# Two head groups of a causal attention accumulated into one bank of outputs through zero-padded value columns

## The chip, the cores and the metric

One core of a Trainium2 chip runs the whole kernel. The metric is the device time of one execution in microseconds (us), the median of three runs.

## The reference

A block of four batches of 512 tokens with 128 features. After a layer norm two branches are added to the input: an attention over chunks of 16 tokens (local and dilated), called the local attention below, and a second branch with a low-rank causal attention over all 512 tokens of a batch (16 heads of 8 features) and a mixture of experts. The change is in the causal attention:

```python
k = (kv_lat @ W_ku).reshape(B, S, NH, HH); q = (q_lat @ W_qu).reshape(B, S, NH, HH)
v = (kv_lat @ W_vu).reshape(B, S, NH, HD)
...
scores = jnp.einsum('bqhd,bkhd->bhqk', qq, kk) * scale
scores = jnp.where(causal[None, None], scores, jnp.finfo(scores.dtype).min)
probs = jax.nn.softmax(scores, axis=-1)
y = jnp.einsum('bhqk,bkhd->bqhd', probs, v).reshape(B, S, H)
return y @ W_o
```

## The kernel before, in words

**One list of steps, five engines.** `plan()` writes out one list of 760 steps. Every engine walks this list in order and does its part of each step, so the order of the list is the order of work on each engine; engines wait for each other by semaphores. Lists for the parts (scores, local attention, projections, stacks of queries and keys, experts and so on) are interleaved by `merged`, each spread evenly over stretches given in the table `SPREAD`.

**Banks.** Seven of the eight PSUM banks are in three rings: A (2 banks: score maxima, local scores, the experts' last product), B (3: scores for the exponentials, the experts' first products) and M (2: nearly everything else). A step takes the next bank of its ring and waits until the step that had this bank before has been drained. The eighth, `bank_c`, collects the products of probabilities and values.

**The causal attention.** The 16 heads of a batch go in four groups of four. For a group there are ten S steps (scores into bank A, L1215 and masks L1222; VectorE takes the row maxima, L1068), one SHIFT (the maxima are transposed, L1303, rounded in two parts, L1075 and L1076, and sent by DMA into the query stack), ten E steps (transposed scores into bank B, L1236; ScalarE's exponential into `p_mla`, L886) and four PV steps (L1332, one for each tile of 128 keys). A PV step has four matmuls, one for each head of the group: head m of group g has its own 32 partitions of `bank_c`, and the weights are 32 columns of `v_mla` from the head's nine on (eight values and a one, which gives the softmax's denominator); the other columns of the 32 leave unused rows. E and PV of a group run two groups behind S.

**Output of a group.** After the last PV step ScalarE copies `bank_c` to `oT_mla` (L895). Then, three or four E steps into the next group, comes the step Y: TensorE transposes `oT_mla` in four tiles into a bank M (L1339), VectorE takes the reciprocals of the denominators (L1130) and multiplies (L1131) into `y_mla`, which lies in `lat_room`. TensorE's first PV step of the next group waits for ScalarE's copy (`c_drained`). So there are 16 Y steps, four for each batch. After the fourth come YT (transposes, L1344) and X1 (the output projection, L1349). The values themselves come from step MV: four matmuls (L1283), which ScalarE copies into `v_mla` (L786).

**Which head is in which group.** VectorE lays the weights of queries and keys out in step WF by sixteen small copies (L981 to L985); the head order of the stacks follows from them. Before, group g holds heads 4g to 4g + 3.

**The start.** GpSimd (POOL) clears `half`, `k_part`, `q_part` and sets `v_rows` to one (L676 to L679), then takes the square roots of the first batch's statistics (L665, in `root`), for which it waits for VectorE; VectorE goes on with L955 to L957, L1000, the normalised rows `xr` (L1002), WF, `xn` (L988), L993, L994, and two memsets, of `s_loc` (L996) and of the ones in `v_mla` (L997). GpSimd's next work in the list is L747. ScalarE's first MV drain waits for `ones_set` at 2.

## Time and profile before

| | us |
|---|---|
| median of three runs | 392.73 |
| the three runs | 392.72, 392.73, 394.63 |
| span of the profiled execution, first to last instruction | 387.9 |

The page gives the profiled execution by its span alone; the median stands 4.8 us above that span. PE is TensorE's matmuls, PEld its weight loads, DVE VectorE, ACT ScalarE, POOL GpSimd, SP the engine whose queue issues most DMAs. The span has three parts: a start (to about 64 us), a stretch in which causal attention, local attention and projections of different batches overlap (64 to about 298 us), and the experts (to the end). "Idle before, releaser" tells what ended an engine's idle time.

### The profile page before, as it was taken

The page shows a single profiled execution, that of the slowest core. Times are in us where ns is not written, and L with a number is a line of the kernel's source. Part 1 is how long each engine was busy: PE and PEld are TensorE (multiplying, and loading weights), DVE is VectorE, ACT ScalarE, POOL GpSimd, SP SyncE. Part 2 cuts the span into 40 slices and gives each one's busy share as a digit, 9 for nine tenths or more (in the row PEclk, how much of TensorE's full clock was granted, in tenths as well). Part 3 has the DMA queues.
Part 4 walks back from the last instruction along what each step waited for, and adds up shares of the span by engine and source line. Part 5 has one row for each costly group of instructions (what it writes and reads, how often), then busy time and mean ns, then how long its engine had stood idle before and what let it go on. Part 6 is the DMA issues. An engine that isn't in the chain of part 4 may idle for free.

```text
span 387.9 us, 11664 instructions
## 1 busy us (share of the span) xinstructions
PE 337.9 (87%) x4504; PEld 205.0 (53%) x4504; DVE 286.0 (74%) x720; ACT 224.1 (58%) x545; POOL 122.7 (32%) x148
## 2 busy tenths in 40 slices
PE   5678987898898988998688889878999999999994
PEld 4366654454465445464445455445445755665663
DVE  6987668798666898878679978879623569668644
ACT  4356434676576465664467658656665564746462
POOL 6286407210600472603301400000201365444543
PEclk9988998999999999999999999999999999999998
DMA  8453141333105033350211331206000000000100
GB/s 193 82 197 100 26 155 43 89 56 65 27 22 160 24 69 54 84 167 3 64 41 30 58 65 48 43 6 161 3 2 0 3 0 27 3 28 0 30 0 27
DMA packets 29141, 21.84 MB, mean 56 GB/s; under 512 B 12312, under 2 KB 26008, under 8 KB 29048
## 3 DMA queue, kind: packets, MB, share of 16 engines
q1 hardware_dynamic: 28872, 20.91, 21.9%
q8 instruction: 36, 0.59, 0.6%
q10 hardware_dynamic: 216, 0.20, 0.2%
q14 instruction: 17, 0.14, 0.1%
HBM read 6.81 MB, written 6.19 MB: 34 GB/s over the span
## 4 chain that ended last, share of the span: by engine, by line
PE 48%; DVE 28%; ACT 10%; issue 7%; SPq 3%; DMA 1%; ACTq 1%; POOL 1%; DVEq 0%; POOLq 0%
PE bank_B L1428 11%; DVE neg_max L1068 6%; PE bank_c L1332 6%; PE bank_A L1434 5%; PE bank_B L1236 5%; PE bank_A L1374 5%; ACT p_mla L886 3%; DVE s_loc L1085 2%; DVE row_max L1082 2%; ACT k_diag L830 2%; PE bank_M L1272 2%; SPq L624 1%; PE bank_M L1382 1%; DVE k_diag L1193 1%; PE bank_M L1397 1%
## 5 line engine op out<-in xcount | busy, mean ns | idle before, releaser
L886 ACT ACTIVATE p_mla<-bank_B 128x512 f32<-128x512 f32 (+1 forms) x176 | 94.3, 562 | 62.7 <-PE bank_B L1222 61.9
L1068 DVE TENSOR_REDUCE neg_max<-bank_A 128x1 f32<-128x512 f32 (+3 forms) x176 | 108.6, 637 | 19.5 <-PE bank_A L1222 15.8
L1236 PE MATMUL bank_B<-q_stack,k_stack 54*128 54x512 bf16 (+3 forms) x256 | 63.2, 303 | 10.9 <-DVE neg_max L1068 5.1
L1215 PE MATMUL bank_A<-k_stack,q_stack 52*128 52x512 bf16 (+3 forms) x256 | 63.7, 303 | 0.1
L1428 PE MATMUL bank_B<-xrT,k_diag 128*128 128x512 f32 x128 | 61.7, 600 | 1.2 <-DVE k_diag L1193 1.0
L759 POOL TENSOR_TENSOR x<-x,q_part 128x512 f32<-128x512 f32 x31 | 39.4, 1272 | 61.3 <-ACT q_part L920 43.0
L1332 PE MATMUL bank_c<-p_mla,v_mla 128*32 128x128 f32 (+12 forms) x512 | 47.5, 444 | 5.6 <-ACT p_mla L886 5.5
L1236 PEld LDWEIGHTS bank_B<-q_stack,k_stack 54*128 54x128 bf16 x256 | 19.2, 93 | 54.0 <-issue 23.1
L920 ACT ACTIVATE q_part<-bank_A,expert_w 128x128 f32<-128x128 f32 x108 | 30.8, 368 | 28.8 <-PE bank_A L1434 28.8
L1193 DVE SCALAR_TENSOR_TENSOR k_diag<-k_diag,bank_B 128x512 f32<-128x512 f32 x32 | 22.0, 687 | 31.5 <-ACT k_diag L904 30.3
L1222 PE MATMUL bank_A<-masks 64*128 64x64 bf16 (+2 forms) x352 | 43.1, 202 | 0.0
L1222 PE MATMUL bank_B<-masks 64*128 64x64 bf16 (+2 forms) x352 | 43.1, 201 | 0.0
L1434 PEld LDWEIGHTS bank_A<-k_diag 128*128 128x128 f32 x256 | 32.8, 191 | 14.4 <-issue 14.3
L1222 PEld LDWEIGHTS bank_B<-masks 64*128 64x128 bf16 x352 | 32.7, 96 | 12.6 <-issue 0.3
L1434 PE MATMUL bank_A<-k_diag 128*128 128x128 f32 x256 | 34.0, 276 | 0.7 <-DVEq L1201 0.7
L1222 PEld LDWEIGHTS bank_A<-masks 64*128 64x128 bf16 x352 | 32.9, 96 | 1.7
L1428 PEld LDWEIGHTS bank_B<-xrT,k_diag 128*128 128x128 f32 x128 | 21.4, 191 | 18.4 <-issue 12.0
L665 POOL TENSOR_TENSOR nrm<-nrm,half 128x8 f32<-128x8 f32 (+1 forms) x8 | 10.6, 1330 | 64.0 <-DVE nrm L1144 61.6
L1374 PE MATMUL bank_A<-k_diag,q_part 128*32 128x128 f32 x544 | 21.4, 292 | 3.6 <-DVE neg_max L1068 1.3
L1198 DVE TENSOR_TENSOR k_diag<-bank_B,k_diag 128x512 f32<-128x512 f32 x32 | 22.1, 691 | 1.1
L771 POOL CAST parts<-rot 128x512 bf16<-128x512 f32 x6 | 3.7, 609 | 56.2 <-DVE rot L1049 52.5
L1082 DVE TENSOR_REDUCE row_max<-bank_A 128x32 f32<-128x512 f32 (+1 forms) x20 | 12.7, 635 | 11.6 <-PE bank_A L1374 11.5
(150 smaller groups left out, 568.8 us busy)
## 6 DMA issues: line engine op xcount, KB each, us to landing
v_dram<-v_rows SPq DMA_DIRECT2D x12, 324.0 KB, 3.6
k_stack<-parts SPq DMA_DIRECT2D x48, 64.0 KB
q_stack<-parts SPq DMA_DIRECT2D x45, 64.0 KB
k_diag<-k_part SPq DMA_DIRECT2D x48, 34.0 KB
v_diag<-v_dram SPq DMA_DIRECT2D x32, 45.0 KB, 2.1
v_diag<-v_dram SPq DMA_DIRECT2D x32, 36.0 KB, 2.1
v_dram<-v_rows SPq DMA_DIRECT2D x4, 283.5 KB, 2.8
x<-in_x SPq DMA_DIRECT2D x4, 256.0 KB, 8.0
```

The lines of the kernel that those rows point to most:

```text
L759: link(nc.gpsimd.tensor_tensor(x[:, tb, :], x[:, tb, :], weighted[down_no[step] % 2], ALU.add))
L886: drained_by(nc.scalar.activation(p_of(n)[:, m:m + len(heads), 0:w], src, ACT.Exp, scale=SCALE), step)
L920: ins = nc.scalar.activation(weighted[n % 2][:, i, :], down[:, i, :], ACT.Copy, scale=expert_w[:, c * NT + i, e - 1:e])
L1068: drained_by(nc.vector.tensor_reduce(neg_max[:, g, m:m + len(heads), i], src, AX.X, ALU.max, negate=True), step)
L1193: drained_by(nc.vector.scalar_tensor_tensor(out=hid[n % 2], in0=gate[n % 2], scalar=1.0, in1=bank_of(step + (0,))[:], op0=ALU.add, op1=ALU ...
L1215: return nc.tensor.matmul(bank_of(step)[:, n * w:(n + 1) * w], q_stack[b % 2][rows, h % 8, i * P:(i + 1) * P], k_stack[b % 2][rows, h % 8, ...
L1222: return nc.tensor.matmul(to, half_eye[half, low, :], triangle[half, :].unsqueeze(1).broadcast_to((SLOT, len(heads), SLOT)), start=False, ...
L1236: nc.tensor.matmul(bank_of(step)[:, m * w:(m + 1) * w], k_stack[b % 2][rows, h % 8, j * P:(j + 1) * P], q_stack[b % 2][rows, h % 8, j * P: ...
L1332: last = nc.tensor.matmul(bank_c[32 * m:32 * m + width, j * P:], heads[:, first:first + width], p_of(n)[:, m, 0:S - j * P], start=(j == 0) ...
L1374: last = nc.tensor.matmul(bank[PAIR * j:PAIR * j + PAIR, c:c + P], q_part[:, a, pair, :], k_diag[:, a, :, CHUNK * pair:CHUNK * pair + CHUN ...
L1428: full_by(nc.tensor.matmul(bank_of(use)[:], w_exp[:, e, m, :], x2T[:, c, :], start=True, stop=True), use)
L1434: last = nc.tensor.matmul(bank[:, i * D:(i + 1) * D], hid[n % 2][:, i * P:(i + 1) * P], w_exp[:, e, 2, :], start=True, stop=True)
```

## The change

The 16 heads are regrouped: group g holds heads g, 4 + g, 8 + g and 12 + g, by another reading order in the sixteen copies of WF. Each head has 18 columns in `v_mla`: nine zeros, its eight values and a one (and one more cell of zeros at the end). Groups 0 and 1, and groups 2 and 3, now accumulate in one `bank_c`. The weights of an even group start at the head's values, so that its result is in rows 0 to 8 of the 32 partitions; those of an odd group start at the nine zeros, so that its result is in rows 9 to 17, and each adds zeros to the other's rows. ScalarE's copy and the step Y are done after the odd group only: 8 in place of 16, each with 32 reciprocals and 256 products a partition in place of 16 and 128. The even Y steps are filtered out after `merged`, so the other steps keep their order; the ring M is dealt out anew without them. GpSimd zeroes `v_mla` (2 x 4 x 17 x 18 = 2448 floats a partition) and sets 128 ones behind its first square roots; VectorE's memset of ones goes.

```diff
-    steps += merged(*lists)
+    steps += [step for step in merged(*lists) if step[0] != "Y" or step[2] % 2]
...
-        v_mla = sb("v_mla", [P, 2, NT, H, HD + 1])
+        v_mla = sb("v_mla", [P, 2, NT, H + 1, 2 * (HD + 1)])
...
+        y_places = lat_room[:, 0:NT * D].rearrange("p (n r) -> p n r", r=PV_WIDTH)
-        rden_mla = sb("rden_mla", [P, H])
+        rden_mla = sb("rden_mla", [P, 2 * H])
...
             root(1, range(1))
+            nc.gpsimd.memset(v_mla[:], 0.0).then_inc(v_mla_zeroed, 1)
+            pool.wait_ge(v_mla_zeroed, 1)
+            nc.gpsimd.memset(v_mla[:, :, :, 0:H, 2 * HD + 1:], 1.0).then_inc(ones_set, 1)
...
-                    drain(step, v_mla[:, b % 2, :, :, 0:HD], bank[:].rearrange("p (i h d) -> p i h d", i=NT, h=H))
+                    drain(step, v_mla[:, b % 2, :, 0:H, HD + 1:2 * HD + 1], bank[:].rearrange("p (i h d) -> p i h d", i=NT, h=H))
...
-                elif kind == "PV" and step[3] == NT - 1:
+                elif kind == "PV" and step[3] == NT - 1 and step[2] % 2:
                     _, b, g, _ = step
                     act.wait_ge(pv_done, pv_no[step])
-                    if g != GROUP_ORDER[0]:
-                        wait_full(act, ("Y", b, GROUP_ORDER[GROUP_ORDER.index(g) - 1]))
+                    if g == 3:
+                        wait_full(act, ("Y", b, 1))
                     elif b:
-                        wait_full(act, ("Y", b - 1, GROUP_ORDER[-1]))
+                        wait_full(act, ("Y", b - 1, 3))
                     nc.scalar.copy(oT_mla[:], bank_c[:]).then_inc(c_drained, 1)
...
-                    ku, qu, rq = (bank[:, 64 * n:64 * n + 64].rearrange("p (e a d) -> p e d a", e=2, d=HH) for n in range(3))
+                    ku, qu, rq = (bank[:, 64 * n:64 * n + 64].rearrange("p (m e b d) -> p e d b m", m=4, e=2, d=HH)
+                                  for n in range(3))
...
-                    nc.vector.memset(v_mla[:, :, :, :, HD:], 1.0).then_inc(ones_set, 1)
...
                     link(nc.vector.reciprocal(den, o[:, :, :, HD]))
+                    c = HD * (g - 1)
                     drained_by(nc.vector.tensor_tensor(
-                        y_mla[:, :, 4 * HD * g:4 * HD * g + 4 * HD].rearrange("p i (h d) -> p i h d", h=4), o[:, :, :, 0:HD],
-                        den.unsqueeze(3).broadcast_to((P, NT, 4, HD)), ALU.mult), step)
+                        y_places[:, :, c:c + 2 * HD].rearrange("p n (a d) -> p n a d", a=2), o[:, :, :, 0:HD],
+                        den.unsqueeze(3).broadcast_to((P, H, 2, HD)), ALU.mult), step)
...
-                    if j == 0 and n > 1:
-                        pe.wait_ge(c_drained, (n - 1) // NT)
+                    second = g % 2
+                    if j == 0 and not second and n > 1:
+                        pe.wait_ge(c_drained, (n - 1) // (2 * NT))
                     heads = v_mla[:, b % 2, j].rearrange("p h d -> p (h d)")
                     for m in range(4):
-                        first = (HD + 1) * (4 * g + m)
-                        width = min(PV_WIDTH, H * (HD + 1) - first)
+                        first = (HD + 1) * (2 * (4 * m + g) + 1 - second)
+                        width = min(PV_WIDTH, 2 * (HD + 1) * (H + 1) - first)
                         last = nc.tensor.matmul(bank_c[32 * m:32 * m + width, j * P:], heads[:, first:first + width],
-                                                p_of(n)[:, m, 0:S - j * P], start=(j == 0), stop=(j == NT - 1),
+                                                p_of(n)[:, m, 0:S - j * P], start=(j == 0 and not second),
+                                                        stop=(j == NT - 1 and second == 1),
                                                 skip_group_check=True)
```

## Rows read from the trace of the kernel before

**Rows 1.** The page's part 1: busy us, share of span, instructions.

```profile
PE 337.9 (87%) x4504; PEld 205.0 (53%) x4504; DVE 286.0 (74%) x720; ACT 224.1 (58%) x545; POOL 122.7 (32%) x148
```

**Rows 2.** Busy time of PE, PEld, DVE, ACT, POOL by stretch; clock, DMA share, GB/s.

```profile
64.00:282.00 218.00, 189.33 (x3404) 110.30 (x3404) 176.17 (x450) 135.00 (x326) 49.57 (x71) 0.99 0.25 61
302.00:388.00 86.00, 79.97 (x376) 49.92 (x374) 54.71 (x125) 47.77 (x143) 40.44 (x32) 0.99 0.04 13
```

**Rows 3.** The page's part 4: the chain that ended last, by engine.

```profile
PE 48%; DVE 28%; ACT 10%; issue 7%; SPq 3%; DMA 1%; ACTq 1%; POOL 1%; DVEq 0%; POOLq 0%
```

**Rows 4.** Who waited for whom: us in total, times, longest us.

```profile
PEld bank_B L1236 <- DVE neg_max L1068: 20.4, 43, 1.5
```

**Rows 5.** Instructions by line and form: busy us, mean ns, idle before.

```profile
L1085 DVE TENSOR_TENSOR s_loc<-bank_A,row_max 128x512 f32<-128x512 f32 x16 | 11.1, 692 | 0.5
...
L1339 PE MATMUL bank_M<-eye,oT_mla 128*128 128x128 f32 x64 | 10.3, 284 | 0.9 <-ACT pT_loc L867 0.8
...
L895 ACT COPY oT_mla<-bank_c 128x512 f32<-128x512 f32 x16 | 9.3, 583 | 0.5 <-PE bank_c L1332 0.5
...
L1096 DVE RECIPROCAL rden<-bank_M 128x32 f32<-128x32 f32 x16 | 5.6, 349 | 0.4 <-DVE s_loc L1085 0.2
...
L1131 DVE TENSOR_TENSOR lat_room<-bank_M,rden_mla 128x128 f32<-128x128 f32 x16 | 4.7, 292 | 0.6
...
L1130 DVE RECIPROCAL rden_mla<-bank_M 128x16 f32<-128x16 f32 x16 | 4.0, 249 | 7.0 <-PE bank_M L1339 6.8 <-DVE s_loc L1085 0.2
```

**Rows 6.** The same view: matmuls of values with 32 and with 9 columns.

```profile
L1332 PE MATMUL bank_c<-p_mla,v_mla 128*32 128x512 f32 x104 | 17.0, 605 | 0.6 <-ACT p_mla L886 0.6
...
L1332 PE MATMUL bank_c<-p_mla,v_mla 128*9 128x512 f32 x8 | 4.1, 596 | 0.0
```

**Rows 7.** The chain that ended last, in order of time: start us, us, what.

```profile
79.86 0.59 PE bank_M L1339 x4
...
144.73 0.17 DVE rden_mla L1130
...
144.93 0.30 DVE lat_room L1131
...
283.91 0.58 ACT oT_mla L895
```

**Rows 8.** Timeline of POOL in the start: start us, us, instruction, idle before.

```profile
1.98 1.92 POOL L678 MEMSET q_part<- 128x2176 f32 x1
3.95 1.18 POOL L679 MEMSET v_rows<- 128x1296 f32 x1
5.71 1.66 POOL L665 TENSOR_TENSOR nrm<-nrm,half 128x8 f32<-128x8 f32 x1 [0.58 <-DVE nrm L949]
15.82 1.15 POOL L747 TENSOR_TENSOR rest<-rot,parts 128x512 f32<-128x512 f32 x1 [8.46 <-ACT parts L841]
```

**Rows 9.** Timeline of DVE in the start.

```profile
4.71 0.44 DVE L947 TENSOR_SCALAR nrm<-mv 128x4 f32<-128x4 f32 x1
...
7.61 0.17 DVE L956 TENSOR_SCALAR nrm<-nrm 128x4 f32<-128x4 f32 x1
...
12.88 0.17 DVE L997 MEMSET v_mla<- 128x128 f32 x1
```

**Rows 10.** Timeline of all engines near 322 us, its rows of POOL and DVE.

```profile
321.78 1.26 POOL L759 TENSOR_TENSOR x<-x,q_part 128x512 f32<-128x512 f32 x1 [0.71 <-ACT q_part L917]
321.85 0.18 DVE L1150 RECIPROCAL nrm<-nrm 128x4 f32<-128x4 f32 x1
...
322.07 1.26 DVE L1152 TENSOR_SCALAR xn<-x,nrm 128x128 f32<-128x128 f32 x2
```

**Rows 11.** Line L1152 alone: ns min/median/max, first and last start us.

```profile
L1152 DVE TENSOR_SCALAR xn<-x,nrm x16: 274/279/1061, 163.8 to 323.4; 128x128 f32<-128x128 f32 x16
```

**Rows 12.** Columns as in rows 2: two stretches of 2 us in the start.

```profile
22.00:24.00 2.00, 0.58 (x5) 0.33 (x6) 0.93 (x7) 1.33 (x3) 1.81 (x4) 0.99 0.43 129
24.00:26.00 2.00, 2.00 (x10) 2.00 (x11) 1.81 (x3) 0.14 (x2) 1.65 (x5) 0.50 0.51 151
```

More of the change, by code:

```diff
@@ L461, in build @@
         ones_set = sem("ones_set")
+        v_mla_zeroed = sem("v_mla_zeroed")
         pT_cleared = sem("pT_cleared")
@@ L975, in _, with to @@
                     wait_full(dve, step)
-                    ku, qu, rq = (bank[:, 64 * n:64 * n + 64].rearrange("p (e a d) -> p e d a", e=2, d=HH) for n in range(3))
-                    rk = w_ropek.rearrange("p (e a) d -> p e d a", e=2)
+                    ku, qu, rq = (bank[:, 64 * n:64 * n + 64].rearrange("p (m e b d) -> p e d b m", m=4, e=2, d=HH)
+                                  for n in range(3))
+                    rk = w_ropek.rearrange("p (m e b) d -> p e d b m", m=4, e=2)
+                    def to(n, d0, d1, e):
+                        return w_mla[:, n, d0:d1, :, e].rearrange("p d (b m) -> p d b m", m=4)
                     part = HH // 2
@@ L980, in _ @@
                         for side, plain, turn in ((0, ku, rk), (1, qu, rq)):
[L981 to L985 removed]
+                            nc.vector.tensor_copy(to(side, 0, HH, e), plain[:, e])
+                            nc.vector.tensor_copy(to(side, HH, HD, e), turn[:, e])
+                            nc.vector.tensor_copy(to(2, HH * side, HH * side + part, e), turn[:, e, part:])
+                            nc.vector.tensor_copy(to(2, HH * side + part, HH * side + HH, e), turn[:, e, 0:part])
                     drained_by(nc.vector.tensor_copy(w_mla_v[:], bank[:, 192:192 + D]), step)
@@ L1120, in _ @@
                 elif kind == "Y":
-                    g, n = step[2], GROUP_ORDER.index(step[2])
-                    o = bank[:].rearrange("p (i h r) -> p i h r", i=NT, h=4)
+                    g = step[2]
+                    o = bank[:].rearrange("p (n r) -> p n r", r=PV_WIDTH)[:, :, 0:2 * (HD + 1)].rearrange(
+                        "p n (a c) -> p n a c", a=2)
                     wait_full(dve, step)
-                    if n:
-                        wait_drained(dve, ("Y", b, GROUP_ORDER[n - 1]))
+                    if g == 3:
+                        wait_drained(dve, ("Y", b, 1))
                     elif b:
                         wait_full(dve, ("YT", b - 1))
-                        wait_drained(dve, ("Y", b - 1, GROUP_ORDER[-1]))
-                    den = rden_mla[:].rearrange("p (i h) -> p i h", i=NT)
+                        wait_drained(dve, ("Y", b - 1, 3))
+                    den = rden_mla[:].rearrange("p (n a) -> p n a", a=2)
                     link(nc.vector.reciprocal(den, o[:, :, :, HD]))
+                    c = HD * (g - 1)
                     drained_by(nc.vector.tensor_tensor(
-                        y_mla[:, :, 4 * HD * g:4 * HD * g + 4 * HD].rearrange("p i (h d) -> p i h d", h=4), o[:, :, :, 0:HD],
-                        den.unsqueeze(3).broadcast_to((P, NT, 4, HD)), ALU.mult), step)
+                        y_places[:, :, c:c + 2 * HD].rearrange("p n (a d) -> p n a d", a=2), o[:, :, :, 0:HD],
+                        den.unsqueeze(3).broadcast_to((P, H, 2, HD)), ALU.mult), step)
                 elif kind == "X1":
@@ L1336, in _ @@
                 elif kind == "Y":
-                    pe.wait_ge(c_drained, b * (H // 4) + GROUP_ORDER.index(step[2]) + 1)
+                    pe.wait_ge(c_drained, 2 * b + step[2] // 2 + 1)
                     for i in range(NT):
```

4 lines of the change are left out of this document (removed).

## The prediction

> **What bounds the kernel now.** I read the page's busy shares first, then the busy time by stretch, then the chain that ended last, and last the rows of the instructions that the change touches. The reader is to see that no engine is full over the span, TensorE nearest to it at 87% [rows 1]. Between 64 and 282 us TensorE is busy 189.3 of 218 us, VectorE 176.2 and ScalarE 135.0; in the experts (302 us on) TensorE has 80 of 86 us and the others some 50 [rows 2]. The chain lies to 48% on TensorE, 28% on VectorE and 10% on ScalarE [rows 3]: in the overlapped stretch TensorE and VectorE hand the bound to and fro, as the weight loads of E show, which waited 20.4 us for VectorE's maxima in 43 places [rows 4]. So neither engine's saving counts in full; what counts is what lies on the chain, and whether the other engine's saving falls at the same place.
>
> **What is removed in the overlapped stretch.** Eight Y steps and the copies before them.
> TensorE: 64 transposes kept it busy for 10.3 us in union [rows 5]; half is 5.2 us (0.65 us a step). The matmuls of values keep their number; for the last heads some had 9 to 27 columns of weights and now all have 32, and the rows give 605 ns against 596 [rows 6], so nothing: eight narrow ones at 9 ns more are 0.1 us.
> ScalarE: 8 copies of 583 ns, 4.7 us [rows 5].
> VectorE: a Y costs 249 + 292 = 541 ns, two cost 1.08 us. After, one costs a reciprocal of 32 elements, 349 ns by L1096, and a product of 256. Between 128 elements (292 ns) and 512 (692 ns, L1085) a straight line gives 292 + 128 x 1.04 = 425 ns. That is 0.77 us for a pair, so 0.31 us is saved, 2.5 us for eight [rows 5]. The new output has gaps of 16 floats and its input gaps in the bank; L1131's had both, so I add nothing, and 10% more would be 0.3 us in all.
> The wait of TensorE's first PV for the copy goes in eight places, and in ring M each step after a removed Y now waits for an older one. I found no place where the first wait ended an idle time, and the second is bounded by 0 and about 1 us; I take 0.3.
>
> **How much of it is on the chain.** I went through the chain around each of the eight. Three removed Ys have their transposes on it, 0.59 us each (one of the three is the piece at 79.86), 1.8 us. Three have VectorE's two instructions on it, 0.17 + 0.30 and the handovers, about 0.5 us each (one is the pair at 144.73 and 144.93), 1.5 us. A seventh, near 267 us, has 0.4 us of VectorE, and the eighth has the copy at 283.91, 0.58 us. Sum 4.3 us [rows 7]. The eight Ys that stay are longer by 0.77 - 0.54 = 0.23 us; three of them have this same pair of instructions on the chain, 0.7 us back. So the chain gets 3.6 us shorter. Other paths run close to it: VectorE alone is relieved by 2.5 us only, TensorE alone by 5.2. I take 3.3 us, with the 0.3 of ring M in it, and keep 2.0 and 5.5 (TensorE's 5.2 and a bit of ring M) as the ends. The experts after 302 us are unchanged and only start earlier; TensorE is nearly full there [rows 2], so nothing is given back.
>
> **What is added in the start.** ScalarE's copies into `v_mla` and WF's sixteen copies keep their sizes, only strides change: nothing, at worst 0.2 us. VectorE loses a memset of 0.17 us [rows 9], which lies on its unbroken row of work: 0.17 us gained. GpSimd gets two memsets behind its square roots. From 2176 elements in 1.92 us and 1296 in 1.18 [rows 8] comes 0.84 ns an element and 0.09 fixed, so 2448 elements take 2.15 us. They start at about 7.44 (the roots end at 5.71 + 1.66 = 7.37) and end at 9.6; the 128 ones end by 9.9. GpSimd's next work is at 15.82, after 8.46 us idle [rows 8], so for GpSimd and for the wait of the first MV drain this is hidden.
> It is not hidden for VectorE. In the start L947, a tensor_scalar of four elements, took 0.44 us where the like L956 took 0.17 [rows 9]; it began at 4.71 and ended at 5.15, just behind GpSimd's memset of `v_rows`, which ended at 3.95 + 1.18 = 5.13 [rows 8]. The same near 322 us: GpSimd's L759 runs from 321.78 to 323.04. A reciprocal beside it took its 0.18 us, but two tensor_scalars of L1152, begun at 322.07, took 1.26 [rows 10]; one of this line took 1061 ns where the median is 279 [rows 11], and 322.07 + 1.06 is 323.13. So a tensor_scalar from SBUF to SBUF that comes during an instruction of GpSimd waits for its end, while a reciprocal does not. In the new kernel L956 comes at 7.61, 0.17 us into the memset. It then ends at 9.6 in place of 7.78, 1.8 us late, and all that follows on VectorE to 20 us (the rows `xr`, WF, `xn`, the rotations) is one unbroken row of work in the chain. ScalarE, TensorE and GpSimd wait for it there, so the start gets longer by 1.8 - 0.17 = 1.7 us, rounded up. The low end is the stretch that L947 itself showed, 0.44 - 0.17 = 0.27 us, less the 0.17: 0.1. The high end adds a memset that takes longer than the line, 2.2 us.
> The Trainium skill states this as a rule (SBUF — State Buffer, section Who interferes with whom): an instruction of VectorE in a mode with two ports, which tensor_scalar can enter, shares a port pair with GpSimd, and the one that comes second is fully blocked until the other is done. By this rule the added time is the whole rest of the memset and the start 1.7 us longer; were rows 9 only a slow first instruction, the sum would be 1.6 us better. The trace agrees with the rule in both places.
>
> **Sum.** 392.7 - 3.3 + 1.7 = 391.1; in the profile, a span of 387.9 - 1.6 = 386.3 us, with the same 4.8 us around it by which the median stands above the span. I say **391.0**. A change of 0.5%, 2.0 us, is about what a measurement of this kernel can tell from none, so the bounds are 390.8 and 394.7.
>
> **The rivals.**
> *The start costs nothing* (the memset begins late or between VectorE's instructions, or the delay is taken up later): 392.7 - 3.3 - 0.2 = 389.2. For it: nothing in the rows but a chance of timing; if VectorE came first, L1002, also a tensor_scalar and three instructions later, would meet the memset and wait the same. Chance 0.12.
> *TensorE is the bound everywhere*: its whole 5.2 us and 0.3 of ring M count, with the start as above: 392.7 - 5.5 + 1.7 = 388.9. For it, 87% busy in the stretch; against it, the 20.4 us of waits for VectorE. Chance 0.15.
> *VectorE is the bound in the stretch*: only its 2.5 us count, less some for rows on its own that wait: 392.7 - 2.0 + 1.7 = 392.4. Chance 0.20.
> *Slower: the late start lets TensorE's clock fall.* Behind a stretch of 2 us with 0.58 us of matmuls the granted clock went to 0.50, its lower level of 1.2 GHz, for the next 2 us [rows 12]. TensorE now waits 1.8 us longer before the transposes of `xr`. If the clock falls there, the first transposes and the four projections of 512 columns behind them run at half speed and, as VectorE waits for each, cost up to 2 us; later dips of the same kind, at other places than now, could cost 2 us more. With the low saving: 392.7 - 2.0 + 1.7 + 3 = 395.4. It decides once the clock costs more than 2.3 us over the low saving, or 3.6 over mine. Against it: before those steps TensorE runs warm-up matmuls and the clock holds now through comparable gaps. Chance 0.08.
> That the change does not do what it says (the steps stay) can be left out: the Y steps are filtered from the list.
>
> **How the numbers follow.** My forecast has 0.45, with its own range of 390.0 to 392.3; a third of that lies below 390.8. Faster by over 0.5%: 0.12 + 0.15 + 0.15 of the forecast's 0.45 = 0.42. Slower: 0.07 of the last rival, which can also end short of the bound. Same: the rest, 0.51. The range of 388.6 to 393.0 takes in the first three rivals and leaves out the last and the tails of the others.
>
> **What would show it.** Right: 32 instructions each on L1339's successor (half of 64), 8 copies to `oT_mla` with 583 ns, reciprocals of 128x32 near 350 ns and products of 128x256 near 425; a tensor_scalar of about 2 us on VectorE at 7.6 us beside a GpSimd memset of 2.15 us, and the first rotation (L1017) at about 14.6 in place of 12.9; the experts start some 1.6 us earlier, and from there the two kernels are alike. Wrong: L956 at 0.17 us with the memset beside it; TensorE's idle time between 64 and 298 us growing by as much as its work shrinks (then it was VectorE's bound); a granted clock below 1.0 before 20 us; PV matmuls slower than 605 ns; ScalarE's first copy into `v_mla` waiting for the ones.

## The result and the profile after

| kernel | median us | runs | mean clock |
|---|---|---|---|
| before, measured beside it | 393.68 | 4 | |
| changed | 400.74 | 4 (398.13 to 404.38) | 0.956 |
| ratio to before | 1.0174, 95% interval 1.0087 to 1.0260 | | |

The changed kernel is slower by 1.7% in these runs. The forecast was 391.0 in a range of 388.6 to 393.0. Here and below a ratio leaves out the slow runs, those more than 1.5% above the quickest run of their kernel, while a mean is over all runs, since the runs of one kernel spread here without a step.

The page after: busy time, the granted clock in 40 slices, and the chain by engine.

```profile
PE 346.9 (87%) x4472; PEld 206.8 (52%) x4472; DVE 285.8 (72%) x703; ACT 221.5 (56%) x537; POOL 125.1 (31%) x150
...
PEclk9996999999699998999999989999979999999998
...
PE 47%; DVE 22%; SPq 11%; ACT 8%; issue 6%; POOL 3%; DMA 2%; DVEq 0%; ACTq 0%; POOLq 0%
```

Against [rows 1]: TensorE has 32 matmuls fewer and yet 9.0 us more busy time, which is a lower clock and not more work. Against [rows 3]: VectorE's share of the chain went from 28% to 22%, and that of SPq, the time in which SyncE issues DMAs one after another, from 3% to 11%. The span is 397.6 us, the execution 399.42.

The changed lines, by form:

```profile
L1352 PE MATMUL bank_M<-eye,oT_mla 128*128 128x128 f32 x32 | 5.2, 285 | 0.8 <-ACT pT_loc L872 0.8
L900 ACT COPY oT_mla<-bank_c 128x512 f32<-128x512 f32 x8 | 4.7, 581 | 0.5 <-PE bank_c L1344 0.5
L1142 DVE TENSOR_TENSOR lat_room<-bank_M,rden_mla 128x256 f32<-128x256 f32 x8 | 3.4, 424 | 0.3
L1140 DVE RECIPROCAL rden_mla<-bank_M 128x32 f32<-128x32 f32 x8 | 2.8, 350 | 3.5 <-PE bank_M L1352 3.3 <-DVE s_loc L1094 0.2
L791 ACT COPY v_mla<-bank_M 128x512 f32<-128x512 f32 x4 | 2.6, 656 | 6.9 <-PE bank_M L1294 6.9
```

All the work that the change removes is gone, and the forecasts of 349 and 425 ns hold. Only the copy into `v_mla`, with 72 bytes from head to head in place of 36, took 656 ns where before's (its L786) took 586: 0.3 us for four, forecast at 0 to 0.2.

The start, POOL's and then DVE's timeline:

```profile
7.42 2.14 POOL L684 MEMSET v_mla<- 128x2448 f32 x1
9.62 0.33 POOL L686 MEMSET v_mla<- 128x128 f32 x1
```

```profile
7.40 0.18 DVE L960 RECIPROCAL nrm<-nrm 128x4 f32<-128x4 f32 x1 [1.84 <-POOL nrm L667]
7.61 1.97 DVE L961 TENSOR_SCALAR nrm<-nrm 128x4 f32<-128x4 f32 x1
9.62 0.18 DVE L962 RECIPROCAL nrm<-nrm 128x4 f32<-128x4 f32 x1
```

The tensor_scalar of four elements was held for 1.97 us, to the memset's end, as forecast. The Trainium skill (SBUF — State Buffer, section Who interferes with whom) says that of a GpSimd instruction and a VectorE instruction in a mode with two ports, which tensor_scalar can enter, the one that comes second is fully blocked; this trace agrees, with 1.97 us in place of the 0.17 of [rows 9].

Behind that the changed kernel's profiled execution loses more than forecast. The second instruction of each SHIFT (L1076, after it L1085) marks the progress of the overlapped stretch; it starts at these times in the profiled executions (us from the start; e1 is the first experiment below):

```
SHIFT number        1      3      4      5      6      10      16    span
before          48.04  78.88  90.14 100.89 117.70  186.82  276.18   387.9
changed         51.17  82.03  92.72 105.01 123.42  193.43  283.00   397.6
e1              48.72  79.64  90.33 102.50 119.67  188.96  281.40   396.0
```

The changed kernel is 3.1 us late at the first SHIFT, not 1.7; then, where the forecast had it catch up by 3.3 us, it falls back by another 3.7 to the sixteenth, and by 2.9 from there to the end, where the granted clock is low between 292 and 300 us.

One pair of executions can't give the start's price, though. The transposes of `xr` come at 11.20 to 11.24 us in all four profiles with the memset (changed, e2, e3, e8) and at 9.39 to 9.69 in the fourteen without it: 1.8 us that the memset surely costs. The first SHIFT comes at 48.7 to 55.3 us (mean 51.6) in the four, and at 45.9 to 53.2 (mean 49.9) in the fourteen.

**Which execution the forecast stood on.** In nearly all executions measured since, of before too, the time is 1.8 us above the span (399.42 and 397.6 here; up to 2.4 in one kernel). The 4.8 us between before's span and its median were thus most likely not time around the span: that execution will have been one of some 389.7 us (387.9 + 1.8), at a mean clock of 0.984, while 63 runs of the kernel before, those beside e1 to e8, e13 and e14, had a mean of 394.2 at 0.973 and reached from 388.6 to 402.8 (with the 18 runs beside the other experiments the mean is 394.0). So a profile says where time goes in one execution; small differences need means over many.

### The profile page after: what moved, and what is told of

Same layout as the page of the kernel before. It is cut to its first block, busy times and chain, and to the rows that moved or that the text cites. A ratio compares the mean times of both kernels' runs of the same rounds, so it can differ in the third digit from the quotient of the medians.

```text
span 397.6 us, 11553 instructions
## 1 busy us (share of the span) xinstructions
PE 346.9 (87%) x4472; PEld 206.8 (52%) x4472; DVE 285.8 (72%) x703; ACT 221.5 (56%) x537; POOL 125.1 (31%) x150
## 4 chain that ended last, share of the span: by engine, by line
PE 47%; DVE 22%; SPq 11%; ACT 8%; issue 6%; POOL 3%; DMA 2%; DVEq 0%; ACTq 0%; POOLq 0%
PE bank_B L1441 11%; PE bank_c L1344 6%; SPq L542 5%; PE bank_A L1447 5%; SPq L626 5%; PE bank_B L1247 5%; DVE neg_max L1077 5%; PE bank_A L1387 4%; ACT p_mla L891 3%; PE bank_M L1283 2%; DVE s_loc L1094 2%; DVE row_max L1091 2%; DMA q_stack<-shift 2%; PE bank_M L1288 1%; PE bank_M L1278 1%
## 5 line engine op out<-in xcount | busy, mean ns | idle before, releaser
L1247 PE MATMUL bank_B<-q_stack,k_stack 54*128 54x512 bf16 (+3 forms) x256 | 65.5, 312 | 12.2 <-DVE neg_max L1077 5.3
L1226 PE MATMUL bank_A<-k_stack,q_stack 52*128 52x512 bf16 (+3 forms) x256 | 66.0, 312 | 2.0 <-DVE neg_max L1077 2.0
L1441 PE MATMUL bank_B<-xrT,k_diag 128*128 128x512 f32 x128 | 63.7, 615 | 0.9 <-DVE k_diag L1204 0.8
L1344 PE MATMUL bank_c<-p_mla,v_mla 128*32 128x128 f32 (+3 forms) x512 | 49.2, 457 | 6.2 <-ACT p_mla L891 6.2
L1233 PE MATMUL bank_A<-masks 64*128 64x64 bf16 (+2 forms) x352 | 44.4, 206 | 0.0
L1233 PE MATMUL bank_B<-masks 64*128 64x64 bf16 (+2 forms) x352 | 44.3, 206 | 0.0
L1233 PEld LDWEIGHTS bank_B<-masks 64*128 64x128 bf16 x352 | 33.6, 98 | 13.8 <-issue 1.9
L1233 PEld LDWEIGHTS bank_A<-masks 64*128 64x128 bf16 x352 | 33.8, 98 | 2.2 <-issue 0.8
L1226 PEld LDWEIGHTS bank_A<-k_stack,q_stack 52*128 52x128 bf16 x256 | 19.4, 94 | 5.5 <-DVE neg_max L1077 2.2
```

The costliest lines, as they stand in the source:

```text
L1226: return nc.tensor.matmul(bank_of(step)[:, n * w:(n + 1) * w], q_stack[b % 2][rows, h % 8, i * P:(i + 1) * P], k_stack[b % 2][rows, h % 8, ...
L1233: return nc.tensor.matmul(to, half_eye[half, low, :], triangle[half, :].unsqueeze(1).broadcast_to((SLOT, len(heads), SLOT)), start=False, ...
L1247: nc.tensor.matmul(bank_of(step)[:, m * w:(m + 1) * w], k_stack[b % 2][rows, h % 8, j * P:(j + 1) * P], q_stack[b % 2][rows, h % 8, j * P: ...
L1344: last = nc.tensor.matmul(bank_c[32 * m:32 * m + width, j * P:], heads[:, first:first + width], p_of(n)[:, m, 0:S - j * P], start=(j == 0 ...
L1441: full_by(nc.tensor.matmul(bank_of(use)[:], w_exp[:, e, m, :], x2T[:, c, :], start=True, stop=True), use)
```

## The experiments

Changed and before differ by about 6 us in their means. The theories were: **the start** (memset, and what the late start does), **the removal** is worth less than forecast since something else ends the waits (SP's queue), **the layout** (padded columns) costs, and **the clock** falls more often where TensorE has less to do. Means are given with their standard errors, and ratios with their 95% intervals against runs of before on the same chip. I read differences of a few us from the means, with 394.2 +- 0.4 for before (63 runs). The experiments ran in five groups, each on a chip of its own with runs of before beside it, whose means were 393.4 (e1 to e4), 394.4 (e5 to e8), 392.5 (e9 to e12), 395.1 (e13, e14) and 393.8 (e15, e16), with errors of 0.5 to 0.8. Against its own group e1 is 2.1 +- 0.9 us over before, e2 4.2 +- 1.2, e7 1.6 +- 1.0 and e8 5.9 +- 1.4.

### e8_changed_again: the changed kernel once more

No edit.

> The changed kernel once more, for its spread beside the others. All theories: 398 to 402, and 3 to 6 us above the first run's kernel.

Median 400.48 (13 runs, 393.97 to 407.73, mean 400.3 +- 1.2, clock 0.959), ratio 1.0070 (1.0003 to 1.0137). Slower again; the two ratios, 1.0174 and 1.0070, show how far few runs of this kernel carry. The mean is 6.1 +- 1.3 over before's.

### e1_scalar_zero: the change without GpSimd's memset

```diff
-            nc.gpsimd.memset(v_mla[:], 0.0).then_inc(v_mla_zeroed, 1)
...
+            nc.scalar.memzero(v_mla[:].rearrange("p s j h c -> p (s j h c)")).then_inc(v_mla_zeroed, 1)
...
+                    dve.wait_ge(v_mla_zeroed, 1)
+                    nc.vector.memset(v_mla[:, :, :, 0:H, 2 * HD + 1:], 1.0).then_inc(ones_set, 1)
```

> The changed kernel, but ScalarE zeroes v_mla in its idle time behind its two clears, and VectorE sets the ones where the kernel before did, so that no GpSimd memset meets VectorE's tensor_scalar. Theory A (the loss is the late start and what it does to TensorE's clock there, later dips are chance): the tensor_scalar takes 0.17 us again, the start is as before and the time is 3 us under the kernel before, about 390. Theory B (less work on TensorE lets its clock fall more often): the start is as before, but dips near 102, 153, 231 and 293 us stay, and the time is 395 to 398.

Median 395.72 (12 runs, mean 395.5 +- 0.7, clock 0.966), ratio 1.0070 (1.0024 to 1.0116). The first SHIFT comes at 48.72, 0.7 us behind before. So by the means the memset on GpSimd costs 400.3 - 395.5 = 4.8 +- 1.4 us of the changed kernel; a line through each kernel's runs, read at the same clock of 0.975, gives 395.5 - 392.9 = 2.6 us, so that nearly half of it is clock. Against each one's own group of runs it is 5.9 - 2.1 = 3.8 +- 1.6. The ratios, 1.0070 for both kernels, show no difference at all. What is left is still above before by 1.3 +- 0.8 us, without the memset: the removal does not pay. At the clock of 0.975 before stands at 393.4, e1 0.5 us under it.

### e2_before_late: the kernel before with only the memset

```diff
+        room = sb("room", [P, 2448])
...
             root(1, range(1))
+            nc.gpsimd.memset(room[:], 0.0).then_inc(room_zeroed, 1)
+            pool.wait_ge(room_zeroed, 1)
```

> The kernel before with one GpSimd memset of 2448 floats into a room of its own behind the first square roots; nothing else changed. Theory A: VectorE's tensor_scalar takes 2.0 us, the first score step is 3 us later and the time is 3 us or more above the kernel before, 396 to 400, with the same dips moved or added as in the changed kernel. Theory B: 1.8 us slower and no new dips after 60 us, 394.5 to 396.

Median 398.24 (12 runs, mean 397.6 +- 1.1, clock 0.968), ratio 1.0059 (1.0006 to 1.0113), by the means 3.4 +- 1.2 us over before. DVE's and PE's timelines in its start:

```profile
7.61 1.97 DVE L960 TENSOR_SCALAR nrm<-nrm 128x4 f32<-128x4 f32 x1
```

```profile
11.20 1.11 PE L1271 MATMUL bank_M<-eye,xr 128*128 128x128 f32 x4 [2.75 <-DVE xr L1006]
12.11 1.06 PE L1252 MATMUL bank_c<-eye 128*128 128x128 f32 x4
13.25 3.75 PE L1281 MATMUL bank_M<-xrT,w_mla 128*128 128x512 f32 x4
```

The kernel before had for the same three 0.66, 0.61 and 1.96 us. TensorE sat idle for 2.75 us before the transposes of `xr`, where it was 0.93, and then ran at half speed; the granted clock is below 1.0 from 10 to 18 us. The first SHIFT is at 51.36, 3.3 us late, and every later interval is that of before within 0.1 us: the sixteenth is at 279.47. So in this execution the start costs 1.8 us of blocked VectorE and another 1.5 of slow TensorE, and both persist. This is the last rival's first half, at its place and near its price ("up to 2 us"). But TensorE is also slow there in nine of the fourteen profiles without the memset (e1's lines stand at the end): the transposes of `xn`, which follow these projections, come at 18.0 to 19.2 us in the four profiles with it (mean 18.9) and at 15.8 to 17.3 in the fourteen without (mean 16.2; before 15.79). On average that is 1.8 us and another 0.8.

### e7_left_out: the removal without the layout

The kernel before with its own values, weights and banks; the even Y steps and the copies before them are left out and the odd ones take two groups' size, so the results of groups 0 and 2 are lost.

```diff
+    steps += [step for step in merged(*lists) if step[0] != "Y" or step[2] % 2]
...
-                    if j == 0 and n > 1:
-                        pe.wait_ge(c_drained, (n - 1) // NT)
+                    if j == 0 and g % 2 == 0 and n > 1:
+                        pe.wait_ge(c_drained, (n - 1) // (2 * NT))
```

> The kernel before with its own layout of values and heads; the copies and Y steps of groups 0 and 2 are left out (the results of these groups are lost), those of groups 1 and 3 have the changed kernel's larger form. So it has the whole saving and nothing of the padding. Theory C: as the first run, 394 to 397, since neither has the new wait lifted. A theory E, that the padded layout costs time by itself (copies into v_mla, weights of 32 columns, another order of heads): 390 to 392.

Median 395.62 (12 runs, mean 395.9 +- 0.8, clock 0.968), ratio 1.0061 (0.9999 to 1.0124): the same as e1 within 0.4 +- 1.0 us. Padded columns, strides, regrouped heads and ScalarE's zeroing cost nothing that can be told; leaving the steps out is by itself worth nothing, or less. The line through e7's runs stands at 394.3 at the clock of 0.975, 0.9 us over before's, where e1's is 0.5 under: the removal's worth at equal clock is nil within this scatter.

### e3_filler and e4_zero_filler: TensorE's work put back alone

In place of each removed Y four products of `eye` with itself go into a bank of ring M, drained by VectorE's queue without an instruction; once in the changed kernel, once in e1.

```diff
+                elif kind == "FILL":
+                    for i in range(NT):
+                        last = nc.tensor.matmul(bank[:, i * P:(i + 1) * P], eye[:], eye[:], start=True, stop=True)
+                    full_by(last, step)
```

> The changed kernel with four products of the unit matrix with itself on TensorE, into a bank of ring M, in the place of each Y that was removed; nothing reads them. Theory B: TensorE is kept busy as before, the clock's dips behind 90 us go, and the time falls to 393 to 396 although TensorE has more to do. Theory A: nothing changes in the dips, the time stays at 400 or grows by up to 3 us.

> Both edits: zeroes by ScalarE and the filler on TensorE. Only ScalarE's copies and VectorE's part of the removed Ys are then saved. Theory A: between the kernel before and the first run, 391 to 392. Theory B: 391 to 392 too, but below the first run. If the first run is faster than this one, the removed transposes are worth their time.

Medians 398.47 (6 runs, mean 399.4 +- 1.1, clock 0.973) and 399.26 (6, 399.5 +- 0.7, 0.967). In the changed kernel the products cost nothing (399.4 against 400.3), in e1 they cost 4.0 +- 1.0 us. So it isn't that TensorE merely needs to be kept busy: the profiles still have falls of the clock, e3's at 194 us and e4's at 100. Why the products cost e1 so much isn't shown; that at the old places they lay on the chain is my reading. The two kernels differ only in where `v_mla` is zeroed, and here GpSimd's memset costs nothing: 399.4 against 399.5, -0.1 +- 1.3 us.

### Where the removal's gain went

e1 against before by intervals between SHIFTs (us, from the same marks; the last column adds up to e1's 4.46 us more from the third SHIFT to the sixteenth):

```
interval   before     e1   difference   granted clock in e1
3 to 4      11.26  10.69     -0.57      full
4 to 5      10.75  12.17     +1.42      falls at 100
5 to 6      16.81  17.17     +0.36      low until 104
6 to 10     69.12  69.29     +0.17      full
10 to 11    18.93  20.73     +1.80      falls at 195
11 to 14    41.55  41.65     +0.10      full
14 to 15    18.74  20.15     +1.41      falls at 253
15 to 16    10.14   9.91     -0.23      full
```

Two things are in it, SP's queue and the clock. Where the clock stays full, the sum of the differences is -0.5 us: that is what the removal of some seven Y steps was worth at equal clock (0.66 us from SHIFT 12 to 13 went the other way, and e7 has the same 17.12 us there, e1 17.11, before 16.45).

The queue shows first behind SHIFT 4. SP's timeline with the DMAs of the second and the fourth SHIFT, and TensorE's wait for the latter, in before and then in e1:

```profile
65.56 1.20 SPq L632 DMA_DIRECT2D q_stack<-shift  x2
94.57 1.21 SPq L632 DMA_DIRECT2D q_stack<-shift  x2
98.13 0.37 PE L1236 MATMUL bank_B<-q_stack,k_stack 54*128 54x512 bf16 x1 [1.07 <-DMA q_stack<-shift]
```

```profile
66.23 1.20 SPq L634 DMA_DIRECT2D q_stack<-shift  x2
95.23 1.21 SPq L634 DMA_DIRECT2D q_stack<-shift  x2
99.11 0.37 PE L1247 MATMUL bank_B<-q_stack,k_stack 54*128 54x512 bf16 x1 [1.85 <-DMA q_stack<-shift]
```

Between the two SP issues DMAs with no pause over 0.11 us, and the distance is 29.0 us whether the Y steps are there or not (29.00 also in changed and in e2, 29.02 in e7). e1 had gained 0.57 us from SHIFT 3 to 4 and lost it, and more, in that wait: 0.8 of the 1.42 us from SHIFT 4 to 5 are before the clock falls. The transposes at 79.86 in [rows 7] lay on the chain, and yet leaving them out could gain nothing here, since behind them the chain of before runs through this queue, from 83.86 to 95.15 us.

The stretch from 6 to 10 holds four batch-quarters of work and gained nothing. Its chain, e1 from 134 us on (in order of time, us):

```profile
148.24 0.69 SPq L626
...
148.97 0.69 SPq L626
...
149.69 0.64 SPq L542
150.38 0.65 SPq L542
...
151.07 0.61 SPq L542
...
151.72 0.58 SPq L634
...
152.35 2.69 DMA q_stack<-shift
...
155.17 0.37 PE bank_B L1247
```

These are the last of an unbroken row that begins at 134.63. SP issues the DMAs of key stack, query stack and `k_diag` at 0.61 to 0.75 us each, one after another; the SHIFT's two, for which VectorE's last instruction ran at 142.7, go at 151.72, and TensorE waits 0.6 us for their landing. The kernel before has the same row, from SP's timeline:

```profile
139.71 2.05 SPq L540 DMA_DIRECT2D q_stack<-parts  x3
141.81 5.85 SPq L624 DMA_DIRECT2D k_diag<-k_part  x8
147.70 1.99 SPq L540 DMA_DIRECT2D q_stack<-parts  x3
149.73 1.21 SPq L632 DMA_DIRECT2D q_stack<-shift  x2
```

There the SHIFT's instruction ran at 140.66 and its DMAs were issued at 149.73; the row up to there lasts 17.15 us, in e1 17.09. TensorE reached this one late enough, but not by much. Its waits for SHIFT's DMAs in the whole execution (us in total, times, longest), first before, then e1, e7, e11 and e12:

```profile
PE bank_B L1236 <- DMA q_stack<-shift: 1.1, 1, 1.1
```

```profile
PE bank_B L1247 <- DMA q_stack<-shift: 2.4, 2, 1.9
```

```profile
PE bank_B L1240 <- DMA q_stack<-shift: 3.6, 4, 2.0
```

```profile
PE bank_B L1241 <- DMA q_stack<-shift: 5.8, 4, 3.4
```

```profile
PE bank_B L1252 <- DMA q_stack<-shift: 8.0, 4, 3.2
```

Where TensorE comes earlier it waits longer for the same queue.

### e11_before_more and e12_zero_more: more work on SP's queue

Two more DMAs of 1 KB ahead of each SHIFT's, 32 issues in all, in before and in e1.

```diff
+                    for r in range(2):
+                        sp.dma_start(spare[:, 2 * (4 * b + g) + r, :], io["c_eye"][0:4 * NT, 0:16]).then_inc(spare_in, 16)
```

> The kernel before with two more small DMAs on SP's queue (1 KB each, into a spare tile that nobody reads) ahead of those of each SHIFT: 32 issues, some 19 us more of SP's time. Theory C: where SP's queue is full, between the second and the tenth SHIFT above all, intervals grow by up to 1.2 us each, and TensorE waits longer for SHIFT's DMA: 4 to 10 us slower. Theory D: nothing beyond 1 us.

> The same two DMAs in the first run's kernel. Theory C: it ends level with the eleventh run at the same clock, since both are then bound by the same queue: the intervals between SHIFTs in the full stretches differ by under 0.3 us. Theory D: as the first run.

402.31 and 403.19 (2 runs each), ratios 1.0241 (1.0154 to 1.0327) and 1.0263 (1.0184 to 1.0341). 32 issues of 0.60 to 0.70 us are 19 to 22 us on SP, and about 8 us of them come through (402.3 - 394.2; 403.2 - 395.5; for e11 it is 9.9 against its own group's 392.5), in the kernel before too. Not all of this is the wait itself: e11's clock was 0.956, and its profile has some 17 us at the low clock between the first and the last SHIFT, where before's has 3. But in stretches at the full clock its intervals are longer too, from SHIFT 8 to 9 by 1.6 us (14.32 against 12.71) and by 0.4 each from 3 to 4 and from 7 to 8. So this queue is at the bound in places and next to it in others, in both kernels. With it lengthened, the removal is worth nothing again, within an error of 1.3 us.

### e9_before_kd_pool and e10_zero_kd_pool: less work on SP's queue

GpSimd issues the sixteen `k_diag` DMAs of a batch in place of SP, in before and in e1.

```diff
-                            sp.dma_start(view(k_diag[rows, 0, places[0], :],
...
+                                pool.dma_start(view(k_diag[rows, 0, places[0], :],
```

> The kernel before with the 16 DMAs for k_diag of each step KD (batches 1 to 3) issued by GpSimd, which already waits for the same local scores there, instead of by SP. SP has 48 issues of 0.7 us less. Theory C (SP's queue of issues is next to the bound before the change and is the bound after it): the waits of TensorE for the DMAs of SHIFT go (1.1 us before), and in stretches at the full clock the intervals between SHIFTs get shorter by 0 to 3 us in all; if GpSimd's issues are dear, the local scores wait instead. Theory D (the clock alone): intervals at the full clock as before.

> The first run's kernel with the same edit. Theory C: its intervals between SHIFTs at the full clock are 0.3 to 1 us shorter for each removed Y than those of the ninth run, and its time is 1 to 4 us under the ninth run's. Theory D: the intervals at the full clock differ from the ninth run's by under 0.2 us, as those of the first run from the kernel before did.

400.32 (4 runs, ratio 1.0172, 1.0106 to 1.0238) and 399.63 (5 runs, 1.0175, 1.0115 to 1.0235). TensorE's waits for the SHIFT's DMA are gone from both profiles, and from the third SHIFT to the sixth, where neither clock falls, e10 takes 37.14 us and e9 38.21: with the queue out of the way the removal is worth 1.1 us there, where with it e1 was 1.2 us behind before (clock included); the forecast was 3.3 for the whole. The DMAs of the second and fourth SHIFT are then 24.9 us apart in e9, in place of 29.0. But GpSimd pays for it, in e9 its timeline shows

```profile
143.56 2.22 POOL L720 DMA_DIRECT2D k_diag<-k_part  x4 [0.29 <-POOL q_part L729]
```

four times over, 0.55 us a DMA, and the interval from SHIFT 7 to 8, where most of them stand, took 18.45 us in e9 and 19.66 in e10 against before's 14.61, some of it by a fall of the clock in it. The bound only moved.

### e5_zero_shift_act and e6_before_shift_act: a miss

```diff
+                elif kind == "SHIFT":
...
+                    for r in range(2):
+                        act.dma_start(q_stack[b % 2][row + r:row + r + 1, a0:a0 + 4, :].rearrange("o a (i n) -> o (a i) n", n=P),
+                                     shift[:, r, :]).then_inc(shift_in[g], 16)
```

> The first run's kernel (zeroes by ScalarE), and the two small DMAs of each step SHIFT, from shift into q_stack, are issued from ScalarE's queue, no longer from SP's behind its batches of DMAs for k_diag and the stacks. Theory C (the removed Ys save nothing between 64 and 280 us because SP's queue of issues, which they leave as it is, became the bound): against the same edit of the kernel before this kernel saves 2 to 4 us, where without the edit it was no faster than the kernel before. Theory D (TensorE's clock alone eats the saving): the two kernels with this edit stand as those without, this one 1 to 3 us slower.

> The kernel before with the DMAs of SHIFT issued from ScalarE's queue. Theory C: SP's queue is only just off the bound here, so 0 to 3 us faster than the kernel before, less ScalarE's time for 32 issues. Theory D: no difference beyond ScalarE's issues, 0 to 2 us slower.

422.9 and 419.3 us, ratios 1.0625 (1.0506 to 1.0744) and 1.0640 (1.0576 to 1.0705). ScalarE's own waits in e6:

```profile
ACT p_mla L886 <- issue: 16.1, 12, 2.2
```

In before there is no such line. As I read it, ScalarE is held in its own order by the SHIFT, with the exponentials queued behind it. With a clock of 0.925 and 0.937 the two kernels are some 26 us slower, with and without the removal, which tells nothing of SP's queue.

### The clock

The second thing in the table: three falls within the stretch cost e1 some 1.0, 1.6 and 1.4 us. (Of the 1.42 and 0.36 us beside the first, 0.8 is the wait for the DMA; of the 1.80 beside the second, 0.24 is there at the full clock too, as changed and e12 show with 19.18 and 19.17 us.) At 195 us the place can be read; the windows of before, then of e1 (columns as in [rows 2]):

```profile
188.00:190.00 2.00, 2.00 (x100) 1.63 (x90) 1.36 (x3) 0.47 (x1) 0.00 (x0) 1.00 0.11 26
190.00:192.00 2.00, 0.74 (x17) 0.42 (x4) 1.62 (x6) 0.00 (x1) 0.00 (x0) 1.00 0.42 110
192.00:194.00 2.00, 1.27 (x14) 1.12 (x14) 0.11 (x1) 0.58 (x1) 0.00 (x0) 1.00 0.40 77
194.00:196.00 2.00, 2.00 (x29) 0.93 (x26) 1.47 (x3) 1.47 (x4) 0.00 (x0) 1.00 0.44 89
```

```profile
190.00:192.00 2.00, 2.00 (x94) 1.64 (x96) 1.36 (x3) 0.63 (x2) 0.00 (x0) 1.00 0.07 13
192.00:194.00 2.00, 0.63 (x33) 0.54 (x20) 1.72 (x6) 0.00 (x0) 0.00 (x0) 1.00 0.42 114
194.00:196.00 2.00, 1.16 (x9) 0.95 (x8) 0.27 (x2) 0.58 (x1) 0.00 (x0) 0.89 0.33 62
196.00:198.00 2.00, 2.00 (x14) 0.92 (x17) 1.16 (x2) 0.64 (x2) 0.00 (x0) 0.50 0.37 72
```

It is the end of a batch, where TensorE waits for the last Y's product (before 1.14 us, e1 1.37 by PE's timeline), transposes, waits for a copy (0.84) and goes on to X1. The Y that stays is 0.23 us longer, as forecast, and stands just before this gap. In e1 the granted clock then goes to 0.50, the lower level of 1.2 GHz; in before it stayed at 1.00. Before's windows there are nearly as thin, so this pair doesn't show why. At 100 us TensorE had 1.02 and 0.89 us of work in two windows of 2 us in e1, and 0.83 and 1.87 in before, whose wait was shorter. In all, the clock is below full for about 10 us of before's profiled execution (and at its end), for some 30 of the changed one's.

The other profiles say how regular this is. From SHIFT 4 to 5 the clock falls in all five profiles with the removal, with SP's queue as it was or longer, and without added products (changed, e1, e7, e8, e12), and not in before, e2, e9 and e10; it falls in e11, the kernel before with the longer queue. So here the fall goes with the wait for the DMA. From 10 to 11 it falls in e1, e7, e8 and e10, not in changed and e12, and in none of before, e2, e9 and e11. Between 64 and 76 us it is the other way: it falls in each of these last four, and with the removal in changed, e1 and e8 only. Behind the last SHIFT (290 to 308 us) it falls in changed, e1, e8 and e10, not in e7 and e12, nor in before, e2, e9 and e11. These are single executions of each kernel: a tendency, not a rule.

### e13 and e14, e15 and e16: products in the gaps

Extra products of `eye` at these places: before YT, X1, an E at 100 us and the E steps of the last group. e13 (on e1) and e14 (on before) put them into the steps' own banks, e15 and e16 those of YT and X1 into `bank_c`, ahead of the wait for a bank.

```diff
+                if kind in ("YT", "X1"):
+                    for _ in range(gap_warm(step)):
+                        nc.tensor.matmul(bank_c[:, 0:P], eye[:], eye[:], start=True, stop=True)
```

> The first run's kernel with products of the unit matrix in TensorE's gaps, each into the bank that the step behind it already owns and overwrites: four ahead of the waits of YT and two of X1 (batches 0 to 2), six ahead of the wait for SHIFT's DMA near 98 us, one in each E step of the last group. Theory F (the removed Ys widened gaps in front of which TensorE's clock now falls, and this gives the rest of the saving back): the falls near 100, 195, 253 and 291 us go, the mean clock rises from 0.966 to 0.975 or more, and the time is 390 to 393, under the first run's 395.7. Otherwise (the falls come by chance wherever they come): clock and time as in the first run, 395 to 397.

> The same products in the kernel before. Theory F: its gaps at these places seldom cost it the clock, so the mean clock rises little (0.975 to 0.98) and the time stays within 1.5 us of the kernel before. If it falls by more than 2 us, the gaps were a cost of the kernel before as well.

> As the thirteenth run, but the products ahead of YT (four) and X1 (three) go into bank_c, which is free there, and ahead of the wait for the step's own bank, so that they lie inside the gap and not behind it; five ahead of SHIFT's DMA near 98 us; one each in the first four E steps of the last group only. Theory F: no falls of the clock near 100, 195 and 253 us, mean clock 0.972 or more, and with the products now hidden 391 to 394. If the products still cost as much as the falls, 396 or more.

> The same products in the kernel before: 392 to 395 by theory F, within 2 us of the fifteenth run, since at an equal clock the removed Ys were worth about 0.5 us between the second and the last SHIFT.

| | median us | runs | mean clock | ratio |
|---|---|---|---|---|
| e13, on e1 | 399.44 | 12 | 0.973 | 1.0092 (1.0044 to 1.0139) |
| e14, on before | 399.90 | 6 | 0.981 | 1.0176 (1.0106 to 1.0246) |
| e15, on e1 | 397.13 | 6 | 0.979 | 1.0106 (1.0051 to 1.0162) |
| e16, on before | 399.08 | 6 | 0.977 | 1.0139 (1.0083 to 1.0195) |

e13's slices of the clock:

```profile
PEclk9995999999999999999999999999999999999998
```

No fall is left between 42 us and the last slice, and the mean clock of e1's runs rises from 0.966 to 0.973 and 0.979. So filling the gaps takes falls away. It does in before as well (0.973 to 0.981 and 0.977), against what was expected of e14: the gaps cost that kernel some clock too. But in all four the products cost more than they return. In e13 those before YT went out only after the wait that they were to fill (1.28 us idle, then 1.16 us of products). In e15 they lie inside it (0.28 us idle), and the interval from SHIFT 10 to 11 is 19.16 us against e1's 20.73, so the cost of e15 arises at other places, which I did not follow. With the same products in both, e13 lies 0.6 +- 1.2 us under e14 by the means and e15 2.1 +- 1.2 under e16: the removal shows a small gain there, of the size of its error. No version beat the kernel before.

## Why the prediction was wrong

**Right.** What bounds the kernel before (PE, VectorE and ScalarE shares), the counts, 349 and 425 ns, no cost of the padded columns that can be told (e7 and e1 agree within 0.4 +- 1.0 us), the memset's collision to the tenth of a microsecond, and its place. Of the signs named beforehand for being wrong, the granted clock below 1.0 before 20 us came in e8, the changed kernel's second profile, and in e2.

**The step that failed: "How much of it is on the chain".** The 4.3 us of [rows 7] were on the chain, but the chain of one execution says what ended last, not how far ahead of the next path it was. The forecast named two other paths, TensorE's and VectorE's own work, and took 3.3. The third, SP's queue, had 3% of the chain [rows 3] and a single wait of 1.1 us, and the forecast has no term for it. Yet it fixes the distance of the second and the fourth SHIFT's DMAs at 29.0 us, removal or not, and by e11 it lies close behind the chain at other places. Measured at equal clock, the removal brings 0.5 us from the third SHIFT to the sixteenth in place of about 3, and 1.1 us in one stretch of it once the queue is relieved. In the stretches where the queue was not relieved and no wait for it is seen, why the rest did not come through stays open. The rival "VectorE is the bound" (2.0) was nearer, for another reason.

**The step that was too small: "What is added in the start".** 1.7 us were forecast and 1.8 came directly. In e2's profile another 1.5 came by TensorE running slow behind its wait, on average over the profiles 0.8. The means say 3.4 +- 1.2 in e2 against before, 4.8 +- 1.4 in changed against e1 and -0.1 +- 1.3 in e3 against e4, together 2.7 +- 0.7.

**The clock, a term the forecast put at nothing.** The last rival, "slower: the late start lets TensorE's clock fall", had the right sign and kind, with a chance of 0.08 and 395.4. It laid the falls to the late start alone, at up to 2 us there and 2 more later; e1 and e7 have them without the memset. Three falls behind the start cost e1 some 4 us in its profiled execution; in the means, e1's clock is 0.007 under before's 0.973, and at the 3 to 3.7 us by which a run's time moves with 0.01 of clock (lines through the runs of e1 and of before) this is 2.1 to 2.6 us. Against it I had written that the clock "holds now through comparable gaps". It did in the one execution that I had, which was at a high clock. And I had priced work removed from TensorE at zero or a gain, where by the mean clocks of e1 and e7 it came with a loss.

**The sum anew,** in the means: removal at equal clock -0.5, the lower clock +2.1 to +2.6 (e1's and e7's means stand 1.3 and 1.7 over before, so one of the two is a bit too large), memset on GpSimd with what it does to the clock +2.7 by the three pairs together or +3.4 by e2. From 394.2 that is 398.2 to 399.3 with e1's and e7's sums, against 400.3 +- 1.2 measured. (The 4.8 us of changed against e1 can't be put in here: they would give the 400.3 back by construction.)

**Open.** The mean clocks of e1 and of before vary from one execution to the next, so the part of the 2 us that belongs to the removal rests on means with errors of 0.4 and 0.7 us. e13 shows that products in the gaps take falls away, not that the longer Y alone brings them. The three pairs for the memset, 4.8 +- 1.4, 3.4 +- 1.2 and -0.1 +- 1.3, scatter more than their errors suggest, and only the 1.8 us of the blocked instruction are shown by themselves. A version in which SP's queue is short and GpSimd's is too was not found.

## What to carry to other kernels

Before counting what a removed step saves, list every queue that the next steps wait for, the DMA-issuing one too, and read how long each command stood ready before it was issued: a queue with 3% of the chain can fix the pace of a whole stretch. Where TensorE's granted clock falls now and then, compare the mean clocks of many runs before calling work taken from TensorE a gain. Zero a buffer on the engine that is idle and shares nothing with the chain, here ScalarE's 2.23 us in place of GpSimd's 2.14, which spares VectorE's 1.8 us at the least.

## What had not been expected of the hardware

- One and the same kernel (before) took 388.6 to 402.8 us in 81 runs, and its time follows the mean granted clock of 0.958 to 0.989: a line through them gives 3.3 us for 0.01 (3.7 through the 63; 3.0 in e1, e2 and e8).
- In the first 16 us TensorE's matmuls can take 1.6 to 1.7 times as long while the record of the granted clock says 1.00. PE's timeline of e1, where before had 1.32, 0.71, and 0.66 us for the same:

```profile
6.63 2.07 PE L1267 MATMUL bank_M<-lat_room 32*128 32x64 f32 x8
8.63 1.22 PE L1259 MATMUL bank_c<-eye 128*128 128x128 f32 x4
9.64 1.06 PE L1278 MATMUL bank_M<-eye,xr 128*128 128x128 f32 x4
```

- These DMAs of stacks and `k_diag` cost 0.58 to 0.75 us of SP's queue each to issue, and those of `k_diag` 0.55 on GpSimd; the landing of a SHIFT's behind a busy queue took 2.69 us, where the median in before is 1.9.
- ScalarE's copy of 512 elements with 72 bytes from group to group took 656 ns, with 36 bytes 586.
